# The LayerNorm sums of a two-layer macaron transformer taken from VectorE and ScalarE at full width to ScalarE alone in quarters, with the residual loops reordered

## The reference

```python
x = x + 0.5 * L0_ffn(layernorm(x))    # 1024 -> 4096 -> 1024, quantized, conv over 3 tokens, silu
x = x + L0_attn(layernorm(x))         # 16 heads of 64, softmax over 2048 keys, bias b_o
x = x + 0.5 * L0_ffn(layernorm(x))
x = x + 0.5 * L1_ffn(layernorm(x))    # gate over 8 experts, experts 0 and 1, output projection
x = x + L1_attn(layernorm(x))         # linear attention, 512 wide, y_t = M q_t, M += v k^T
x = x + 0.5 * L1_ffn(layernorm(x))

def layernorm(x, eps=1e-5):
    m = mean(x, -1); v = var(x, -1)
    return (x - m) / sqrt(v + eps)
```

## Time and profile before

| | |
|---|---|
| median of 3 runs | 6859.51 us (6857.38 to 6882.17) |
| profiled execution, its own time | 6773.4 us |
| span of the profiled execution, slowest core (core 6) | 6771.8 us (all cores 6743.0 to 6771.8) |
| granted TensorE clock, mean | 0.709 of full speed (all cores 0.705 to 0.710) |
| busy: TensorE matmul, VectorE, ScalarE, GpSimd | 47%, 40%, 25%, 7% |
| chain that ended last, by engine | TensorE 25%, VectorE 24%, ScalarE 21%, DMA 18%, issue 10% |

### The profile page before, as it was taken

How to read it: one execution, slowest core, us unless ns; L and a number is a source line. 1 busy time by engine, 2 the same in 40 slices (tenths; PEclk the granted TensorE clock), 3 DMA queues, 4 the chain that set the end, 5 groups by cost and what they waited for, 6 DMA issues and landing times.

```text
span 6771.8 us, 54149 instructions; the slowest of 8 cores (6743.0 to 6771.8 us)
## 1 busy us (share of the span) xinstructions
PE 3202.6 (47%) x13046; PEld 1263.3 (19%) x13238; DVE 2717.0 (40%) x4228; ACT 1666.6 (25%) x2416; POOL 493.6 (7%) x828
## 2 busy tenths in 40 slices
PE   1021265465345555555555541455465356354255
PEld 0010022222111112112211120222222022122022
DVE  3465555555412222122122236555555323334322
ACT  2310011211035664664654500121211100000000
POOL 1332210010000000000000000000000000000000
PEclk7555587788667667667666775787787678676676
DMA  4532322122010000000000010122122020100012
GB/s 137 159 117 79 90 78 75 44 87 69 19 13 7 5 8 10 5 5 10 6 5 7 7 25 31 56 72 72 50 78 66 13 38 13 31 7 7 16 34 62
DMA packets 142957, 290.63 MB, mean 43 GB/s; under 512 B 35106, under 2 KB 42306, under 8 KB 138050
## 3 DMA queue, kind: packets, MB, share of 16 engines
q0 software_dynamic: 129088, 240.38, 13.3%
q1 hardware_dynamic: 13572, 46.77, 2.1%
HBM read 229.01 MB, written 17.25 MB: 36 GB/s over the span
## 4 chain that ended last, share of the span: by engine, by line
PE 25%; DVE 24%; ACT 21%; DMA 18%; issue 10%; DVEq 1%; ACTq 1%; POOLq 0%; POOL 0%; SPq 0%
ACT aE L249 15%; PE Ops L205 4%; PE meps L205 4%; DVE yconv L225 3%; DVE t1tmp L225 3%; DVE aden L243 3%; DMA slg<-wq2s 3%; ACT atmp L249 3%; PE Hps L205 2%; DMA w2sl<-w2h 2%; PE aqkps L205 2%; PE mops L205 2%; ACT ysilu L249 2%; DVE am2p L238 2%; DVE s2bc L238 2%
## 5 line engine op out<-in xcount | busy, mean ns | idle before, releaser
L205 PE MATMUL Hps<-xsc,slg 128*128 128x512 bf16 (+1 forms) x3518 | 684.6, 344 | 1045.6 <-ACT ysilu L249 435.4
L249 ACT ACTIVATE aE<-aA 128x1024 bf16<-128x1024 f32 x512 | 524.3, 1024 | 394.9 <-PE aA L205 293.5
L249 ACT ACTIVATE aE<-asps 128x1024 bf16<-128x1024 f32 x512 | 524.4, 1024 | 391.5 <-PE asps L205 333.6
L205 PEld LDWEIGHTS Hps<-xsc,slg 128*128 128x128 bf16 x3584 | 291.3, 110 | 1441.0 <-issue 1309.0
L205 PE MATMUL Ops<-xsc,slg 128*128 128x512 bf16 x2002 | 474.6, 387 | 155.7 <-DVE xsc L211 80.8
L249 ACT ACTIVATE atmp<-Hps,cbsb,cw2sb 128x512 f32<-128x512 f32 x256 | 199.0, 777 | 1415.9 <-DVE hlsv L233 1380.8
L205 PE MATMUL aA<-aKp,aQp 64*128 64x512 bf16 x1024 | 387.2, 575 | 286.2 <-ACT aE L249 257.0
L205 PE MATMUL asps<-aQ,aK 65*128 65x512 bf16 x1024 | 336.0, 415 | 253.3 <-DMA aQ<-aQp 229.5
L249 ACT ACTIVATE ln_scr<-x_sb 128x2048 bf16<-128x2048 f32 x48 | 91.7, 1910 | 1256.2 <-DVE x_sb L211 488.2
L225 DVE SCALAR_TENSOR_TENSOR t1tmp<-Hps,cw2sb,atmp 128x511 f32<-128x511 f32 (+1 forms) x512 | 247.7, 484 | 349.9 <-ACT atmp L249 322.5
L205 PE MATMUL apps<-aE,avtok 128*65 128x512 bf16 x1024 | 328.0, 403 | 87.3 <-ACT aE L249 46.0
(11 more groups left out here) (182 smaller groups left out, 3835.8 us busy)
## 6 DMA issues: line engine op xcount, KB each, us to landing
slg<-wq1s POOLq DMA_DIRECT2D x128, 512.0 KB, 3.6
slg<-wq2s POOLq DMA_DIRECT2D x128, 512.0 KB, 3.6
w1sl<-w1h POOLq DMA_DIRECT2D x128, 256.0 KB, 3.0
w2sl<-w2h POOLq DMA_DIRECT2D x128, 256.0 KB, 3.1
x_sb<-x SPq DMA_DIRECT2D x8, 1024.0 KB, 5.0
out<-x_sb SPq DMA_DIRECT2D x8, 1024.0 KB, 3.9
ln_rbc<-rowbuf SPq DMA_DIRECT2D x6, 1024.0 KB
ln_mrbc<-rowbuf SPq DMA_DIRECT2D x6, 1024.0 KB
```

The lines of the kernel that those rows point to most:

```text
L205: tp=tile_position: e.matmul(o, l, r, start=a, stop=b, tile_position=tp),
L249: s=scale, a=accum: e.activation(o, i, f, bias=b, scale=s, accum_out=a),
```

## The change

It has five parts.

1. In `emit_ln` the loops are turned round: the four quarters w of the tokens are outside, the 8 channel blocks inside. Each of the 32 steps casts 512 columns and squares 512 columns, both on ScalarE, into a scratch tile `lnscr` of 128 x 1024 that belongs to the whole program, and then issues the two matmuls. The cast of a step waits for the matmuls of the step before (`lnmm`). VectorE has no part in it.
2. The sublayers record after which VectorE instruction each quarter of `x_sb` is final, and hand these four tags to the next `emit_ln` in `res_q`. The cast of a step then waits for the tag of its quarter. In the first LayerNorm there are no tags and the first cast waits for `guard()`. The first matmul waits for `guard()` as before.
3. The three output projections run `for qb` outside and `for dc` inside, and alternate the PSUM halves by dc.
4. In `ffn_l0`, `yconv` becomes another name for `t1tmp`, and `amax2p` for `sv2_bc`.
5. In `attn_l1` the tiles other than `xln` and `yT` are given free before the output projection.

```diff
+        lnscr = sb("lnscr", [128, 1024], BF16)
+        lnmm = {0: 0}
+        res_q = {"tags": None}
...
         def emit_ln(xln, keep=None):
+            ready = res_q["tags"]
+            res_q["tags"] = None
...
-                scr = lsb("ln_scr", [128, 2 * T], BF16)
...
                     g0 = guard()
-                    for dc in range(DC):
-                        cp("vector", scr[:, 0:T], x_sb[:, dc * T:(dc + 1) * T],
-                           wait=(g0 if dc == 0 else [(Spe, Spe.c)]), inc=Sdv)
-                        act(scr[:, T:2 * T], x_sb[:, dc * T:(dc + 1) * T],
-                            AF.Square,
-                            wait=(g0 if dc == 0 else [(Spe, Spe.c)]),
-                            inc=Ssc)
-                        for w in range(T // 512):
+                    for w in range(T // 512):
+                        for dc in range(DC):
+                            xs = x_sb[:, dc * T + w * 512:
+                                      dc * T + (w + 1) * 512]
+                            w0 = [(Spe, lnmm[0])]
+                            if ready is not None:
+                                w0.append(ready[w])
+                            elif w == 0 and dc == 0:
+                                w0 += g0
+                            cp("scalar", lnscr[:, 0:512], xs,
+                               wait=w0, inc=Ssc)
+                            act(lnscr[:, 512:1024], xs,
+                                AF.Square, inc=Ssc)
                             mm(sum_ps[0:1, w * 512:(w + 1) * 512],
-                               ones_bf[:, :], scr[:, w * 512:(w + 1) * 512],
+                               ones_bf[:, :], lnscr[:, 0:512],
                                start=(dc == 0), stop=(dc == DC - 1),
-                               wait=([(Sdv, Sdv.c)] +
-                                     (g0 if dc == 0 else []))
-                               if w == 0 else (), inc=Spe)
+                               wait=[(Ssc, Ssc.c)] +
+                                    (g0 if w == 0 and dc == 0 else []),
+                               inc=Spe)
                             mm(sq_ps[0:1, w * 512:(w + 1) * 512],
-                               ones_bf[:, :],
-                               scr[:, T + w * 512:T + (w + 1) * 512],
+                               ones_bf[:, :], lnscr[:, 512:1024],
                                start=(dc == 0), stop=(dc == DC - 1),
-                               wait=[(Ssc, Ssc.c)] if w == 0 else (), inc=Spe)
+                               inc=Spe)
+                            lnmm[0] = Spe.c
...
-                yconv = fsb("yconv", [128, QT], F32)
+                yconv = t1tmp
...
-                amax2p = fsb("am2p", [128, QT], F32)
+                amax2p = sv2_bc
...
+                        rtags[q] = (Sdv, Sdv.c)
+                    if q == NQ - 1:
+                        res_q["tags"] = list(rtags)
...
-                        for dc in range(DC):
-                            for qb in range(4):
-                                pw = (dc * 4 + qb) % 2
+                        artags = [None] * 4
+                        for qb in range(4):
+                            for dc in range(DC):
+                                pw = dc % 2
...
                                 ev_by[pw] = Sdv.c
+                            artags[qb] = (Sdv, Sdv.c)
+                        res_q["tags"] = artags
...
+                sctx2.close()
```

More of the change, by code:

```diff
@@ L606, in ffn_l0 @@
                 sv2_bc = fsb("sv2bc", [128, QT], F32)
-                amax2p = fsb("am2p", [128, QT], F32)
+                amax2p = sv2_bc
                 slab_cons = [Spe.c, Spe.c]
+                rtags = [None] * NQ
                 memset("vector", Hl[0][:, :], 0.0, wait=guard(), inc=Sdv)
@@ L1341, in moe_l1 @@
                         ev_by = {0: Sdv.c, 1: Sdv.c}
-                        for dc in range(DC):
-                            for qb in range(4):
-                                pw = (dc * 4 + qb) % 2
+                        mrtags = [None] * 4
+                        for qb in range(4):
+                            for dc in range(DC):
+                                pw = dc % 2
                                 for hc in range(DC):
@@ L1367, in moe_l1 @@
                                 ev_by[pw] = Sdv.c
+                            mrtags[qb] = (Sdv, Sdv.c)
+                        res_q["tags"] = mrtags
         def attn_l1():
@@ L1375, in attn_l1 @@
                 emit_ln(xln)
[L1376 to L1379, removed]
                 yT = asb("ly", [128, KVC * T], BF16)
[L1381 to L1384, removed]
+                sctx2 = ExitStack()
+                asb2 = lambda n, s, d: sctx2.enter_context(
+                    nc.sbuf_tensor(uid(n), s, d))
+                qT = asb2("lq", [128, KVC * T], BF16)
+                kT = asb2("lk", [128, KVC * T], BF16)
+                Ktok = asb2("lktok", [128, NT * KV], BF16)
+                Vtok = asb2("lvtok", [128, NT * KV], BF16)
+                S_sb = asb2("ls", [128, KVC * KV], F32)
+                S_bf = asb2("lsbf", [128, KVC * KV], BF16)
+                Am = asb2("lam", [128, 128], BF16)
+                wbuf = asb2("lw", [128, DC * KV], BF16)
                 if True:
@@ L1546, in attn_l1 @@
                         ev_by = {0: Sdv.c, 1: Sdv.c}
-                        for dc in range(DC):
-                            for qb in range(4):
-                                pw = qb % 2
+                        lrtags = [None] * 4
+                        for qb in range(4):
+                            for dc in range(DC):
+                                pw = dc % 2
                                 for kc in range(KVC):
@@ L1572, in attn_l1 @@
                                 ev_by[pw] = Sdv.c
+                            lrtags[qb] = (Sdv, Sdv.c)
+                        res_q["tags"] = lrtags
         def ffn_first():
```

## The result

| | before | changed |
|---|---|---|
| median of 10 runs, us | 6866.18 (6747.56 to 6904.04) | 7146.36 (7063.02 to 7185.84) |
| ratio, 95% interval | | 1.0545 [1.047, 1.062] |
| profiled execution: span of the slowest core, us | 6771.8 | 7143.6 (cores 7085.4 to 7143.6) |
| the same two kernels timed again: ratio | | 1.0454 [1.0388, 1.0521] |

The change makes the kernel clearly slower, as forecast. The forecast in the form of a ratio was 1.0436. The first comparison puts the loss above it (5.45%), the interval of the second (4.54%) takes it in. Runs of one kernel spread over about 2%, and the first ratio takes only those near the shortest, which are seven of the changed kernel's ten (7063.02 to 7160.20) but three of the ten before (6747.56 to 6760.48). The medians of all ten give 1.041, the shortest runs 1.047.

The account below looks back on a forecast made before the run. No engine bounds the kernel; during each LayerNorm its dependent chain is all that runs. Six longer LayerNorms add 298.8 us to the 6859.5 us median, giving 7158 us, stated range 7080 to 7205.

Parts of the forecast that it names:

- The step: Each of 32 LayerNorm steps: cast, square and matmul pair in a chain without overlap, 2.655 us at the lower clock.
- The clock: TensorE in the new LayerNorm loop falls to 1.2 GHz, so a matmul pair takes 1.00 us.
- Rival 1: The same LayerNorm chain with TensorE at 2.4 GHz: +221 us, 7081 us; chance 0.08.
- The tags: At each tagged LayerNorm's start they hide one step's ScalarE part; first pair 1.87 us after the last addition, not 4.30.
- Rival 2: LayerNorm matmuls of the first three quarters overlap the projection: -11 us, 6849 us, not slower; chance 0.02.
- ScalarE pays more: In LayerNorm steps, table switches between cast and square add 493 us (chance 0.02), or a slower cast 29 us (0.04).
- Rival 3: ScalarE costs more per LayerNorm step: table switches, 7650 us, chance 0.02; a 0.78 us cast, 7187 us, chance 0.04.
- The other parts at nothing: Freed VectorE casts, projection order, renamed buffers and freed tiles outside the LayerNorm loop change no time.
- How the numbers follow: Whole-kernel time: the runs' median 6859.5 us plus the LayerNorms' 298.8 gives 7158 us.
- The sum of the range: The forecast's own range for the whole kernel, 7130 to 7200 us, from 0.15 us per step either way.

Follow-up runs that it names:

- e7_idle_matmuls: The changed kernel with four useless matmuls added behind each step's pair in the first three quarters of every LayerNorm; 7017.57 us, ratio to before 1.0341.
- e2_loop_only: The kernel before with only the turned LayerNorm loop, casts on ScalarE and one small scratch tile, no tags; 7080.4 us, ratio to before 1.044.
- e8_overlap: LayerNorms three, five, six issue each quarter's steps between the next quarter's projection matmuls; the others use the wide tile as two halves; 6716.43 us, 0.9894 to before.
- e3_rest_only: The changed kernel with the old LayerNorm loop and its wide scratch tile put back, tags unused; 6799.32 us, ratio to before 0.998.
- e4_two_tiles: The changed kernel with two small scratch tiles used in turn, the first cast waiting for guard(); 6927.52 us, ratio to before 1.0178.
- e5_half_tiles: The kernel before with its wide scratch tile used as two halves in turn, 16 steps of 1024 columns; 6743.83 us, ratio to before 0.9911.
- e6_cast_vector: The changed kernel with each step's cast back on VectorE beside the square, single small tile kept; 6940.06 us, ratio to before 1.0218.
- e1_changed_again: The changed kernel unaltered, timed again beside the kernel before on the same chip; 7117.31 us, ratio to before 1.0454.

## Why the prediction was right and where it fell short

- **The step.** Forecast 2.655 us with tags and 2.60 without; measured 2.65 and 2.58. Its parts were a cast of 0.63 (0.62), gap 0.09, square 0.63 (0.63), hand-over 0.15, pair 1.00 (1.01), hand-over 0.155. The 0.634 us that the prediction reads from the earlier trace rows is not in those rows, which hold weight loads; nothing rests on it but the upper end of the pair's 0.96 to 1.06.
- **The clock.** Forecast at the lower level, and right. In the third LayerNorm the pair falls back from 0.59 to 0.98 us between the first and the second step, behind a gap of 1.63 us, and stays down. So the runs agree with the forecast and not with the rule of the Trainium skill ("TensorE: Matmul & The Clock Gate", section "HAM oscillation — how this bites in real kernels") that the prediction sets beside it. e7_idle_matmuls shows that more work behind each pair would have kept it up; what exactly decides is not shown. Rival 1 is out.
- **The tags.** One step, as forecast; e2_loop_only shows the value, e8_overlap the reason: once the matmuls are issued between the projection's, the overlap is there. Rival 2 needed another order of issue, and the change has none.
- **ScalarE pays more.** No: 619 ns for the cast, 631 for the square, and ten table loads in all, as before. Rival 3 is out.
- **The other parts at nothing.** Shown by e3_rest_only, 0.998 [0.9937, 1.0024].
- **The step that failed** is the last, "How the numbers follow". I took the LayerNorms' 298.8 us for the whole difference of the two kernels, carried the 86 us by which the runs' median stood above the profiled execution from one kernel to the other as a constant, and left the difference between executions out of the range. The LayerNorms did add 296.6 us, and on cores without time at 0.81 the kernels differ by 303. But a comparison carries a second term that I had at zero, the time that dense matmul stretches spend at 0.81 of the clock, and it need not be equal on both sides. In the two profiled executions the slowest cores have 522 and 163 us of it, and the last three stages, where it falls, add 69 us. In the first ratio the seven changed runs have a mean of 7120.7 and the three of before 6752.7, 368 us apart and not 303. So 1.0545 lies above my upper end (7205 / 6859.5 = 1.050), and the second timing, 1.0454, does not. The row was there to be read: an execution 86 us shorter than the median of the same kernel's runs says what executions differ by.
- **The sum of the range** was wrong too. 0.15 us in 192 steps is 29 us, which makes 7129 to 7187 and not 7200.
- **Luck.** That the median of 7146.36 us is within 12 us of the forecast of 7158 owes something to luck: the 6859.5 us that I started from lie 112 us above the shortest run of before, this median 83 us above the shortest of the changed kernel, and another set of runs would have given other excesses.

What stays open: whether the changed kernel is at 0.81 for longer than the kernel before. The changed kernel's two profiled executions had it on all eight cores and on four; before, e2_loop_only, e4_two_tiles and e8_overlap had it on eight, e5_half_tiles and e6_cast_vector on four, e3_rest_only and e7_idle_matmuls on none. The profiles are too few to tell. The second timing gives no sign of it: the median of before lies 62 us above its shortest run, that of the changed kernel 43.

## What to carry to other kernels

A loop that hands one small tile from engine to engine costs the sum of its links, so count them before cutting the tile: here four times as many steps, each with three hand-overs, and a second pass on the same engine turned 35 us into 85. A tag that says data is ready hides nothing where the consumer's instructions stand behind a whole stage in program order; look first at where they are issued. And two halves of the tile already there gave the gain that the reordering was after.

## What the runs showed of the hardware that was not expected

- Adding four useless matmuls behind every pair made the kernel about 1% faster (1.0341 against 1.0454 and 1.044; a LayerNorm 75 us instead of 85), because they held TensorE at 2.4 GHz. Shortening the step with a second tile did not raise it, though TensorE was then busy for 1.01 us of every 1.54 (granted clock 0.50).
- TensorE lost the upper level within 2.2 us of a first pair that still ran at it (0.59 us at 4089.25, 0.98 at 4091.47), with no gap longer than 1.63 us between them; the gap before the first pair was 2.76.
- The column of the granted clock can mislead at the start of a trace. The first record of that clock lies 391 us into this one. In the first LayerNorm the column says 1.00, while the pairs take 1.01 us, the duration of the lower level:

```profile
55.98 1.28 ACT L233 ACT_TABLE_LOAD   x1 [55.98 <-DMA bosb<-bo]
...
58.87 1.01 PE L208 MATMUL ln_ps<-lnscr,onesbf 128*1 128x512 bf16 x2 [58.87 <-ACT lnscr L252]
```

- The 0.81 level comes and goes with the execution, under the same dense matmuls. Of the ten profiled executions two have none of it on any core, three have it on the four cores of one die, five on all eight, for up to 671 us of a core's span. Neighbouring cores (0 and 1, 2 and 3, 4 and 5, 6 and 7) have it in nearly the same stages, the two pairs of a die often in different ones. In e1_changed_again it comes with 31 to 83 us on the span of a core.
